# Output projection by half groups, and a new order of the work around it, in the last stage of a four-layer attention kernel

## The reference

```
h  = rmsnorm(x, ln1_w);  kv = rmsnorm(ctx, ln1_w)
q  = rope(h @ Wq)             # 16 heads of 64
k  = rope(kv @ Wk)            # 4 heads of 64
v  = kv @ Wv                  # 4 heads of 64
p  = softmax(q @ k.T / 8 + mask)
hidden = x + (p @ v) @ Wo                       # "out"
m  = rmsnorm(hidden, ln2_w)                     # "m_in"
out = hidden + (silu(m @ Wgate) * (m @ Wup)) @ Wdown   # "mg", "mu", "md"
```

## Time and profile before

| | |
|---|---|
| time, median of three runs | 534.85 us (534.6 to 535.42) |
| time of the profiled execution | 533.91 us |
| its span, first to last instruction | 532.1 us |
| mean granted clock of TensorE | 0.961 |
| PE busy | 470.0 us, 88% |
| DVE, ACT, POOL busy | 65%, 58%, 55% |
| last stage, from its first scores | from 283.12 us to the end |

### The profile page before, as it was taken

The page is one execution under the profiler, slowest core; times in us unless marked ns, Lnnn a source line. Parts: engine busy times, 40 slices in busy tenths (PEclk is TensorE's granted clock), DMA queues, the critical chain, the costliest instruction groups (busy, mean ns, idle before and its releaser), DMA issues.

```text
span 532.1 us, 17232 instructions
## 1 busy us (share of the span) xinstructions
PE 470.0 (88%) x7014; PEld 378.8 (71%) x7014; DVE 344.0 (65%) x857; ACT 307.6 (58%) x738; POOL 292.2 (55%) x359
## 2 busy tenths in 40 slices
PE   2899999999999999978646979999999999989875
PEld 1577777777777877767535758877788887868664
DVE  6778675777777775344626666858585958757422
ACT  1378777767777777546413556555756556454421
POOL 5466875688877877776554354454353535422300
PEclk9999999999999999988858899999999999999898
DMA  9950000000000000000000000000000000000000
GB/s 292 222 187 3 4 2 2 2 3 2 3 3 2 4 3 2 1 1 1 1 0 1 3 3 1 3 11 2 12 2 12 2 12 2 12 2 12 1 12 10
DMA packets 12278, 11.43 MB, mean 21 GB/s; under 512 B 5160, under 2 KB 10152, under 8 KB 12200
## 3 DMA queue, kind: packets, MB, share of 16 engines
q1 hardware_dynamic: 11624, 9.01, 6.5%
q10 hardware_dynamic: 576, 1.32, 0.7%
HBM read 9.29 MB, written 1.05 MB: 19 GB/s over the span
## 4 chain that ended last, share of the span: by engine, by line
PE 46%; issue 17%; POOL 16%; DVE 12%; ACT 8%; DMA 1%; POOLq 0%; DVEq 0%; ACTq 0%
PE ps L455 7%; PE ps L469 4%; PE ps L437 4%; PE ps L445 4%; POOL probs L1641 3%; PE ps L738 3%; PE ps L628 3%; PE ps L666 3%; POOL rstd L1520 2%; PE ps L636 2%; POOL x_all L1587 2%; PE ps L395 2%; PE ps L500 2%; PE ps L404 2%; PE ps L480 2%
## 5 line engine op out<-in xcount | busy, mean ns | idle before, releaser
L1208 DVE TENSOR_REDUCE negm<-ps 128x8 bf16<-128x512 f32 x96 | 59.6, 684 | 26.4 <-PE ps L437 26.4
L838 ACT ACTIVATE shared<-ps 128x512 f32<-128x512 f32 x96 | 57.2, 601 | 21.0 <-PE ps L455 19.3
L1641 POOL TENSOR_TENSOR probs<-p,rc 128x512 f32<-128x512 f32 x32 | 33.0, 1044 | 53.6 <-DVE rc L1413 53.6
L1593 POOL TENSOR_TENSOR wide<-wide,cv 128x1024 f32<-128x1024 f32 x24 | 45.5, 1895 | 30.4 <-DVE wide L1187 30.4
L455 PE MATMUL ps<-cst,p 128*128 128x128 f32 x384 | 58.8, 276 | 0.4 <-ACT shared L838 0.4
L832 ACT ACTIVATE p<-ps 128x512 f32<-128x512 f32 x96 | 54.5, 596 | 4.2 <-PE ps L445 4.1
L455 PEld LDWEIGHTS ps<-cst,p 128*128 128x128 f32 x384 | 45.2, 141 | 16.1 <-issue 9.5
L1520 POOL TENSOR_TENSOR rstd<-veps,neghalf 128x2 f32<-128x2 f32 x40 | 29.0, 725 | 48.0 <-DVE veps L1232 28.6
L1023 ACT ACTIVATE late<-ps 128x512 f32<-128x512 f32 x32 | 17.4, 594 | 47.4 <-PE ps L761 47.4
L666 PE MATMUL ps<-in_t,wg 128*128 128x256 f32 x128 | 35.0, 424 | 4.4 <-ACT in_t L983 4.4
L666 PEld LDWEIGHTS ps<-in_t,wg 128*128 128x128 f32 x128 | 26.1, 214 | 10.5 <-issue 6.9
(11 more groups left out here) (191 smaller groups left out, 1212.7 us busy)
## 6 DMA issues: line engine op xcount, KB each, us to landing
late<-in_mask_l SPq DMA_DIRECT2D x2, 512.0 KB, 10.9
result<-x_all SPq DMA_DIRECT2D x8, 128.0 KB, 1.8
x_all<-in_x_tok SPq DMA_DIRECT2D x1, 768.0 KB, 7.3
wide<-in_ctx_t SPq DMA_DIRECT2D x1, 768.0 KB, 9.0
rv<-in_rv ACTq DMA_DIRECT2D x1, 768.0 KB, 7.8
wa<-in_wa SPq DMA_DIRECT2D x1, 512.0 KB, 10.6
w<-in_w SPq DMA_DIRECT2D x2, 256.0 KB, 6.6
wq<-in_wq SPq DMA_DIRECT2D x1, 512.0 KB, 7.6
```

What stands on the lines that cost most here:

```text
L838: A_(pt[:, w % 2, r, :], ring_of("p", w, r), ACT.Copy).then_inc(sm["act_pt"], 1)
L1208: V.tensor_reduce(negm[:, n % 4, :], ps[:, S_BANK[r], :].rearrange("p (a k) -> p a k", k=S), AX.X, ALU.max, negate=True).then_inc(sm["dve_ ...
L1593: P.tensor_tensor(r_op[:, w % 2, :, :], k_t[:, w % 2, :].unsqueeze(1).to_broadcast([128, 4, GT]), head_masks.unsqueeze(2).to_broadcast([12 ...
L1641: P.tensor_tensor(probs[:, t % 2, :].rearrange("p (a k) -> p a k", k=S), p3[:, t % 3, :].rearrange("p (a k) -> p a k", k=S), rc3[:, t % 3, ...
```

## The change

The output projection becomes a use of a bank for each unit: `part_out(n)` makes eight products for unit n, `read_out(n)` adds 128 columns, and the table has `out` in both halves, for unit 2r-1 in the first and unit 2r in the second. The last half rounds have a table of their own, `ENDING`. In the first half, `t0` and `t1` come before and behind `in`, ahead of the keys and queries. In the second half `m_in` moves to directly behind the values. On ACT the squares of group r+1 come at the start of the first half round, ahead of the copies of the values' products, in rounds 1 to 6; the scaling `rms` comes ahead of the copy of `l_text`, in all rounds. On POOL the power comes ahead of the probabilities in rounds 1 to 6.

```
         HALVES = (
             (("s0", 0), ("s1", 0), ("pv0", -1), ("pv1", -1), ("l_in", 2), ("md", -2), ("l_text", 2), ("out", -1),
-             ("l_gate", 2), ("in", 1), ("t0", 0), ("k", 1), ("q0", 1), ("q1", 1), ("t1", 0)),
-            (("s0", 0), ("s1", 0), ("pv0", -1), ("pv1", -1), ("kt", 1), ("ks", 1), ("q2", 1), ("q3", 1), ("m_in", -1),
-             ("v", 1), ("mg0", -1), ("mu0", -1), ("l_back", 2), ("t0", 0), ("mg1", -1), ("mu1", -1), ("t1", 0)),
+             ("l_gate", 2), ("t0", 0), ("in", 1), ("t1", 0), ("k", 1), ("q0", 1), ("q1", 1)),
+            (("s0", 0), ("s1", 0), ("pv0", -1), ("pv1", -1), ("m_in", -1), ("kt", 1), ("ks", 1), ("q2", 1), ("q3", 1),
+             ("out", -1), ("v", 1), ("mg0", -1), ("mu0", -1), ("l_back", 2), ("t0", 0), ("mg1", -1), ("mu1", -1), ("t1", 0)),
+        )
+        ENDING = (
+            (("pv0", -1), ("pv1", -1), ("out", -1), ("md", -2)),
+            (("s0", 0), ("s1", 0), ("pv0", -1), ("pv1", -1), ("m_in", -1), ("out", -1), ("mg0", -1), ("mu0", -1),
+             ("mg1", -1), ("mu1", -1), ("t0", 0), ("t1", 0)),
         )
+        UNITS = (*PER_UNIT, "out")
         def half(r, h):
-            uses = [(what, 2 * r + h + d if what in PER_UNIT else r + d) for what, d in HALVES[h]]
-            return [(what, i) for what, i in uses if 0 <= i < (2 * NG if what in PER_UNIT else NG)]
+            steps = (ENDING if (r, h) >= (NG - 1, 1) else HALVES)[h]
+            uses = [(what, 2 * r + h + d if what in UNITS else r + d) for what, d in steps]
+            return [(what, i) for what, i in uses if 0 <= i < (2 * NG if what in UNITS else NG)]
...
-            def part_out(g):
-                pe.wait_ge(sm["pv3e"], GB * (g + 1))
-                for t in range(TG):
-                    for i in range(8):
-                        ins = mm(bank_of("out", g)[:, t * 128:t * 128 + 128], a3_t[:, g % 2, i, t * 128:t * 128 + 128],
-                                 wo3[:, i, :], start=(i == 0), stop=(i == 7), skip_group_check=True)
+            def part_out(n):
+                g, u = divmod(n, TG)
+                pe.wait_ge(sm["pv3e"], 2 * (n + 1))
+                for i in range(8):
+                    ins = mm(bank_of("out", n)[:, 0:128], a3_t[:, g % 2, i, u * 128:u * 128 + 128],
+                             wo3[:, i, :], start=(i == 0), stop=(i == 7), skip_group_check=True)
...
# ACT, first_half
                 if older:
                     evac_t3(2 * n - 1)
+                if 1 <= r < NG - 1:
+                    sq3(r + 1)
+                if older:
                     evac_pv3(2 * n - 2)
                     evac_pv3(2 * n - 1)
...
                     exps3(2 * n + 1)
+                if r == 0:
+                    sq3(1)
                 if r + 1 < NG:
-                    sq3(r + 1)
+                    rms(r + 1)
                 if r + 2 < NG:
                     read("l_text", r + 2)
-                if r + 1 < NG:
-                    rms(r + 1)
...
                     read("l_gate", r + 2)
+                if live:
+                    evac_t3(2 * n)
                 if r + 1 < NG:
                     read("in", r + 1)
-                if live:
-                    evac_t3(2 * n)
                 if r + 2 < NG:
                     l2_exp(r + 2)
+                if live:
+                    evac_t3(2 * n + 1)
...
# ACT, second_half
                 if live:
-                    evac_t3(2 * n - 1)
                     evac_pv3(2 * n - 2)
                     evac_pv3(2 * n - 1)
+                if 0 <= r - 1 < NG:
+                    read("m_in", r - 1)
                 if r + 2 < NG:
                     l2_tanh(r + 2)
...
# DVE, first_half
                     smax3(2 * n)
+                if 1 <= r < NG - 1:
+                    rms_mean(r + 1)
+                if live:
                     smax3(2 * n + 1)
+                if r == NG:
+                    read("out", 2 * NG - 1)
+                    m_rms_mean(NG - 1)
                 if 0 <= r - 2:
                     read("md", r - 2)
                 if live:
                     sum3(2 * n)
                     sum3(2 * n + 1)
-                if r + 1 < NG:
-                    rms_mean(r + 1)
-                if 0 <= r - 1 < NG:
-                    read("out", r - 1)
+                if r == 0:
+                    rms_mean(1)
+                if 1 <= r < NG:
+                    read("out", n - 1)
+                    m_rms_mean(r - 1)
                 if r + 2 < NG:
                     l2_max(r + 2)
-                if 0 <= r - 1 < NG:
-                    m_rms_mean(r - 1)
...
# DVE, second_half
                     read("q3", r + 1)
+                if live:
+                    read("out", n - 1)
                 if 0 <= r - 1 < NG:
                     read("mg0", r - 1)
...
# POOL, first_half
                     l2_affine(r + 1)
+                    rms_power(r + 1)
                 if r < NG:
                     probs3(4 * r)
                     probs3(4 * r + 1)
-                if r + 1 < NG:
-                    rms_power(r + 1)
+                if r == 0:
+                    rms_power(1)
```

More of the change, by code:

```diff
@@ L948, in m_sq @@
             def m_sq(g):
-                act.wait_ge(*released("out", g))
+                act.wait_ge(*released("out", TG * g + 1))
                 if g >= 2:
@@ L1021, in evac_pv3 @@
                 if g >= 2 and u == 0:
-                    act.wait_ge(sm["p_use"], filled("out", g - 2))
+                    act.wait_ge(sm["p_use"], filled("out", TG * (g - 2) + 1))
                 A_(a3_t[:, g % 2, :, u * S:u * S + S], bank_of(f"pv{t % 2}", t // 2).rearrange("p (a q) -> p a q", q=S), ACT.Copy)\
@@ L1074, in second_half @@
                     read("ks", r + 1)
-                if 0 <= r - 1 < NG:
-                    read("m_in", r - 1)
-                if r + 1 < NG:
                     read("v", r + 1)
@@ L1082, in second_half @@
                     read("l_back", r + 2)
-                if live:
+                if r < NG - 1:
                     evac_t3(2 * n)
@@ L1086, in second_half @@
                     m_tanh(r - 1, 1)
+                if r == NG - 1:
+                    evac_t3(2 * n)
             for g in range(2, NG):
@@ L1368, in read_k, with read_out @@
                 return ins
+            def read_out(n):
+                return V.tensor_tensor(x_all[:, n, :], bank_of("out", n)[:, 0:128], x_all[:, n, :], ALU.add)
             def read_x(what, g):
@@ L1388, in read @@
                     ins = read_k(g)
-                elif what in ("out", "md"):
+                elif what == "out":
+                    ins = read_out(g)
+                elif what == "md":
                     ins = read_x(what, g)
```

## The result

The changed kernel takes 525.16 us (median of 4, 524.63 to 528.26) against 535.13 (534.6 to 535.49) before: ratio 0.982, 95% interval 0.980 to 0.984. Forecast was 525.5. A second set gave 525.68, ratio 0.982 (0.979 to 0.985).

The account below looks back on a forecast made before the run. PE's own products were taken to bound the middle rounds. Terms 3.3 + 0.35 - 3.8 - 1.5 - 0.4 - 7.3 = -9.35 took the span from 532.1 to 522.75; 1.8 outside it and 0.94 to the median gave 525.5 us, range 523 to 528.

Parts of the forecast that it names:

- What bounds: Middle rounds: PE's own products take 27.6 of 29.27 us; only 1.63 us of waits per round can be won.
- Middle rounds: Rounds 2 to 5: 28.3 us each for 29.27, 0.95 gained per round, 3.8 us in four.
- the fit of the squares: ACT, middle rounds: four squares run from 2.7 to 3.97 us, before the values' copies at 3.98, with nothing to spare.
- the 0.39 us at the gate product: Second half rounds: this wait disappears because `m_in` is made four uses before the gate product.
- Round 1: x 0.3 us later because `out` precedes layer 2's statistics; squares hold copies up by 0.75; 0.35 us lost net.
- Round 0: First half: `l_text` copied behind `rms`, PE stands 5.1 us, gate rows run at the low clock; 3.3 us lost.
- Rival B: Transposes don't bring the clock back: round 0 loses 6.0 us, last gate products slow; 530 us, chance 0.12.
- The end: From unit 15's first scores: 30.4 us for 37.7, 7.3 gained, with `out` of unit 14 in the pause behind `m_in`.
- the clock of the last group: End: last gate products at full clock, 1.85 us of the gain, since PE pauses less around `m_in`.
- Rival C: Middle rounds: `l_text` behind `rms` and early squares put a wait where each was removed; 529.3 us, chance 0.13.
- rival D: ACT: `sq3` ahead of `evac_pv3` delays six rounds when x is late; 537.5 us at 2 us; 0.05 with other slow ways.
- Rival E: Round 0: the pause costs only 1.2 us; 523.4 us, chance counted within the forecast's 0.68.

Follow-up runs that it names:

- yardstick: The changed kernel itself, unedited, timed again in the first set of follow-ups: 525.68 us, ratio 0.982 to the kernel before.
- e1: Changed kernel, but in round 0 alone ACT copies `l_text` ahead of the scaled rows: 523.0 us, ratio 0.976.
- e5: Changed kernel with three unused products on GpSimd ahead of its last two steps of x, rounds 1 to 6: 532.03 us, ratio 0.9935.
- e3: Changed kernel with `m_in` back behind `q3` in rounds 1 to 6, `out` between it and `v`: 526.08 us, ratio 0.9827.
- e9: Changed kernel with the edits of e1 and e6, and in round 0 layer 2's statistics ahead of the add of `out`: 519.71 us, ratio 0.9722.
- e10: Kernel of e9 with 36 unused products in TensorE's pauses of rounds 0, 1, 7 and 8: 518.44 us, ratio 0.9695.
- e2: Changed kernel with squares, mean, power and scaling back in their old places in all rounds, TensorE's new order kept: 537.95 us, ratio 1.0045.
- e6: Changed kernel with `in` made and copied ahead of both transposes `t0` and `t1`: 522.47 us, ratio 0.975.
- e4: Changed kernel with projections of units 14 and 15 both behind `md` in round 8, early copy of `m_in` kept: 527.47 us, ratio 0.985.
- e8: Kernel before with only early squares, mean and power (rounds 1 to 6) and scaled rows ahead of `l_text` (all rounds): 531.86 us, ratio 0.9947.

## Why the prediction was right

By its terms, against the profiles (the changed kernel's first trace, and behind it the yardstick's where it differs):

| term | predicted | measured |
|---|---|---|
| start of the last stage | 283.12 | 283.11; 282.17 |
| round 0, first half | 19.6 | 19.74; 19.56 |
| round 0, second half (`out` hidden) | 10.7 | 10.68 |
| round 1, first half | 15.0 | 15.10; with `out` at the low clock 16.73 |
| round 1, second half | 14.0 | 13.94 |
| rounds 2 to 5, each | 28.3 | 28.27 (14.34 + 13.93) |
| round 6, first half | 13.1 | 13.11 |
| round 7, first half | 9.8 | 9.93 |
| end, from unit 15's scores | 30.4 | 32.4, 32.3; at the high clock 30.7 (e1) |
| span | 522.75 | 526.5; 523.6; 522.8 the fastest |

*What bounds.* That PE's own products bound the middle held: what it loses at waits, read from start to start, went from 1.63 us a round to 0.69 (`t1` at 411.31 to `k` at 412.44, less 0.44), and a round became 1.00 us shorter.

*Middle rounds.* The copies of the values start 3.99 us into the round, x comes at 2.56, `k` starts at 11.67; predicted were 3.98, 2.5 and 11.6. The expected gain of 3.8 us in four rounds is 4.0. e5 showed that the fit of the squares has 0.2 us to spare, and that a delay beyond it goes through. One step had the right size and the wrong cause: the 0.39 us at the gate product come from `out` between `m_in` and `mg0`, not from the early `m_in` (e3).

*Round 1.* Without the clock the size is right: x at 3.54 us for 3.5, the copies of the values held up by 0.83 for 0.75, the gate rows at 9.10 for 9.05. The cause was wrong again: it was not the add of `out` ahead of the statistics that made x 0.3 us later, since without it in that place x is no earlier (e9). And the clock was counted at nothing here; it took 1.6 us in the first trace.

*Round 0.* The loss was predicted at 3.3, and e1 gets 3.4 back in the trace. The pause was 5.31 us for 5.1. In the changed kernel's first trace the granted clock is 0.50 through `t0`, `in` and half of `t1` (297.40 to 299.60), 0.63 from there to `k` and 1.00 from `k` on (0.94 from start to start). In the yardstick's it is 0.60 in `in` and 1.00 in `t1`. So the clock came back while transposes alone were running, after the gate rows and nearly three groups of them, or nearly two. Rival B did not occur, and the rule that the prediction cites from the Trainium skill ("TensorE: Matmul & The Clock Gate", Part 4, PE-mode transpose) finds no support here, though the gate rows ahead of them are matmuls and no run takes the two apart. e10 shows the other side: with the pause filled the same gate rows run at 1.07 for 1.94.

*The end.* The step that was mis-sized is the clock of the last group: "1.85 of it in the last group's clock", called the least certain. It was lost again in the profiled execution (5.38 us for the 16 gate passes, 3.69 at the high clock), and kept in the yardstick's, which lost 1.6 at `out` of unit 15. The reason given was the pauses around `m_in`, 1.6 and 0.3 us; they measured 1.12 and 0.65, and the pause of 1.29 ahead of `out` of unit 15 was not considered. Of the eight traces with the new end and no fillers, three lose clock at one or the other place (both of the changed kernel, and e3) and five at neither (e1, e2, e5, e6, e9). What decides it is open. The chain from the last projection to the gate products, 3.97 us predicted, took 3.97 (510.87 to 514.84). And I gave the credit for the closed pause to unit 14's projection, where e4 shows that moving ScalarE's copy of `m_in` ahead of the exponentials is enough for the first gate products.

*The size.* In the profiled execution the end is 2.0 us over its forecast and the first half of round 1 1.7 over, most of both by the clock; that explains 526.5 for 522.75. The closeness of the median is in part luck. By the mechanism alone the forecast would have been 524.55 (522.75 and the 1.8 us outside the span). The further 0.94 came from the median shown of before, and stood in for clock that the prediction had said would not be lost. In the yardstick's trace this can be followed: the end is 1.9 us over, the last stage starts 0.95 early, in work that the change does not touch, and the span is 523.6, 0.85 over the forecast one.

Rival C (the middle gains nothing) and rival D (slower by `sq3`) did not occur; e5 shows that D is real once x is more than 0.2 us late. Rival E did not occur either.

## What to carry to other kernels

When one engine is saturated, look for each of its waits, read start to start, and ask which of its own later work could stand between the wait's producer and its consumer. That is what splitting `out` did, and the placing of `in` ahead of other transposes did again (e6). Before moving a step ahead of another on a side engine, write down when its input comes in each round, the first one too: the same move that by itself gained 0.62 us in every middle round (e8) cost 3.0 us in round 0 there and 3.4 in the changed kernel, where its producer had not been moved. Parts of a reordering are not worth their single gains: the early squares alone gave 2.4 us, with the loss of round 0 in them, the rest without them and without that loss lost 2.2 against the kernel before, and both together gave 10.0.

## What the runs showed of the hardware

- The clock of TensorE was low after pauses of 1.3 to 2.5 us in one execution and not in another of the same kernel (`out` of unit 15 took 2.02 or 3.65 us after the same pause of 1.29, `out` of round 1 3.28 or 1.96 after pauses of 2.52 and 2.51). With unused products in the pauses the granted clock was 1.00 from 283.12 to 517 us in e10's trace, for 0.98 in e9's (0.980 for 0.967 as the mean over the span).
- Two scalings on VectorE took 1.44 us beside GpSimd's products and 0.60 without them (e5, 405.50, against 429.38 in the kernel after, where GpSimd waits for them). GpSimd's own products took 0.7 us each in both, so only VectorE's work is longer beside them; by which path, no run tells.
